# A decoder kernel whose feed-forward is prepared inside the two stages before it: first weights unpacked and turned there, x normalised batch by batch

## The reference, cut to what matters

```python
x = x + L0_attn(layernorm(x), ...)              # 16 heads of 32, one shared K and V
x = x + L0_xattn(layernorm(x), ctx_1024, ...)   # "the mixing"
x = x + L0_ffn(layernorm(x), gate_up_packed, gate_up_scales, down_packed, down_scales)

def L0_xattn(x, ctx, Wq, bq, Wk, bk):
    query = einsum('bnc,dc->bnd', ctx, Wq) + bq
    key = einsum('bnc,dc->bnd', ctx, Wk) + bk
    attention = softmax(einsum('bnd,bmd->bnm', query, key), axis=-1)
    return einsum('bln,bmn->blm', x, attention)

def L0_ffn(x, gate_up_packed, gate_up_scales, down_packed, down_scales):
    # packed: int32 with 8 four-bit floats each; scales: float16 [in/128, out]
    w_gu = dequant_fp4(gate_up_packed, gate_up_scales)     # [2816, 512]
    w_down = dequant_fp4(down_packed, down_scales)         # [512, 1408]
    gate, up = split(x @ w_gu.T, 1408)
    y = (silu(gate) * up) @ w_down.T
    return y / sqrt(mean(y * y, axis=-1) + EPS)
```

## Time and profile before

| what | value |
|---|---|
| median of 3 runs | 2740.32 us (2739.88 to 2743.84) |
| the profiled execution | 2736.73 us, of it span 2735.0 us |
| mean granted clock of TensorE | 0.952 |
| PE, busy in the span | 2459.4 us (90%) |
| DVE | 1747.2 us (64%) |
| ACT | 1212.6 us (44%) |
| POOL | 157.9 us (6%) |

### The profile page before, as it was taken

How to read it: one execution, slowest core, us unless ns; L and a number is a source line. 1 busy time by engine, 2 the same in 40 slices (tenths; PEclk the granted TensorE clock), 3 DMA queues, 4 the chain that set the end, 5 groups by cost and what they waited for, 6 DMA issues and landing times. The chain is left out here.

```text
span 2735.0 us, 39447 instructions
## 1 busy us (share of the span) xinstructions
PE 2459.4 (90%) x11412; PEld 1779.8 (65%) x11412; DVE 1747.2 (64%) x3684; ACT 1212.6 (44%) x2343; POOL 157.9 (6%) x265
## 2 busy tenths in 40 slices
PE   7999977679999769899999599999999999999579
PEld 5554445457777657654446477777777777777457
DVE  6677756668888662266664666676667666666643
ACT  3566654223333332266663344444444444444321
POOL 0000000010000000100003101010100101010100
PEclk9999998879999979989999799999999999999789
DMA  5522100000000023343320100000000000000101
GB/s 164 167 70 69 52 0 0 17 1 1 0 0 0 4 102 114 120 112 92 84 54 0 54 9 19 4 15 4 15 12 8 12 12 15 4 8 0 40 1 62
DMA packets 71459, 103.69 MB, mean 38 GB/s; under 512 B 14447, under 2 KB 27514, under 8 KB 71262
## 3 DMA queue, kind: packets, MB, share of 16 engines
q1 hardware_dynamic: 71390, 102.82, 12.8%
HBM read 72.90 MB, written 29.88 MB: 38 GB/s over the span
## 5 line engine op out<-in xcount | busy, mean ns | idle before, releaser
L2673 DVE SCALAR_TENSOR_TENSOR x_res<-xa_out_bank,xa_den,x_res 128x512 f32 (+1 forms) x256 | 191.5, 748 | 157.2 <-PE xa_out_bank L2313 157.2
L2582 ACT ACTIVATE xa_pT_hi<-xa_t_bank 128x512 fp32r<-128x512 f32 x256 | 149.5, 597 | 124.8 <-PE xa_t_bank L2450 124.8
L2593 ACT ACTIVATE xa_prob<-xa_prob,xa_nmax 128x512 f32<-128x512 f32 x256 | 182.9, 717 | 30.0 <-DVE xa_nmax L2655 30.0
L2313 PE MATMUL xa_out_bank<-xa_o_w,xa_o_hi 128*128 128x512 f32 x512 | 173.1, 419 | 22.5 <-DVE x_res L2673 20.9
L2637 DVE TENSOR_TENSOR xa_pT_lo<-xa_t_bank,xa_pT_hi 128x512 fp32r<-128x512 f32 x256 | 175.7, 687 | 22.7 <-ACT xa_pT_hi L2582 18.6
L2655 DVE CUSTOM_DVE_ANT_0 xa_prob<-xa_s_bank,xa_mask_bias 128x512 f32<-128x512 f32 x256 | 171.1, 687 | 20.1 <-PE xa_s_bank L2313 10.1
L585 DVE TENSOR_REDUCE l1s_mx<-l1s_max_bank 128x1 f32<-128x512 f32 x256 | 156.3, 682 | 13.2 <-PE l1s_max_bank L447 13.2
L1722 DVE SCALAR_TENSOR_TENSOR ffn_yT<-ffn_y,ffn_ysc,ffn_yT 128x512 f32<-128x512 f32 x176 | 129.3, 748 | 48.9 <-PE ffn_y L1494 48.7
L585 DVE TENSOR_REDUCE l0s_mx<-l0s_max_bank 128x1 f32<-128x512 f32 x256 | 156.0, 682 | 2.8 <-PE l0s_max_bank L447 2.7
L2450 PE MATMUL xa_t_bank<-ident,xa_prob 128*128 128x128 f32 x1024 | 149.8, 274 | 0.1
L572 ACT ACTIVATE l1s_pT<-l1s_score_bank 128x512 f32<-128x512 f32 x256 | 140.0, 601 | 16.3 <-PE l1s_score_bank L466 14.8
(11 more groups left out here) (447 smaller groups left out, 5905.9 us busy)
## 6 DMA issues: line engine op xcount, KB each, us to landing
l0s_q<-l_q SPq DMA_DIRECT2D x96, 128.0 KB, 2.4
l1s_q<-l_q SPq DMA_DIRECT2D x96, 128.0 KB, 3.1
l1s_k<-l_k SPq DMA_DIRECT2D x96, 128.0 KB, 3.3
l0s_k<-l_k SPq DMA_DIRECT2D x96, 64.0 KB, 2.4
x_res<-in_x_dram SPq DMA_DIRECT2D x4, 1024.0 KB, 9.8
l_q<-l_q_hi SPq DMA_DIRECT2D x16, 256.0 KB, 2.6
l_q<-l_q_lo SPq DMA_DIRECT2D x16, 256.0 KB, 3.3
l_q<-l1p_hi SPq DMA_DIRECT2D x16, 256.0 KB, 2.1
```

Of the source, the lines that this page charges most:

```text
L2313: last = pe.matmul(bank, w, x, start=(m == 0), stop=(m == len(pairs) - 1))
L2582: act.activation(pT_hi[:, kt % (QT - 1), :], t_bank[kt % 2][:], ACT.Copy).then_inc(pT_hi_done, 1)
L2593: act.activation(prob[:, q, :], prob[:, q, :], ACT.Exp, bias=nmax[:, q:q + 1], scale=-1.0, accum_out=den[:, r, 0, q:q + 1]).then_inc(exp_d ...
L2673: dve.scalar_tensor_tensor(xt, out_bank[:], den[:, r, 2, q:q + 1], xt, ALU.mult, ALU.add)\
```

## The change

It touches everything from the attention's start to the end of the feed-forward's chunk 0, and nothing behind.

- The feed-forward has no preparation stage. Its packed weights are loaded by SP during the attention's projections. Its scales are loaded turned, element by element, by eight DMAs in ACT's own instruction stream, ahead of the first exponential: four of 128x22 and four of 128x11 two-byte values. The 48 small products and the casts are gone.
- Chunk 0 is unpacked by DVE in the attention: four instruction pairs in each of the head pairs 2 to 5 (they cover magnitudes and signs), exponents and scale tables at pair 24, values at 25, signs put in at 29; ACT scales the weights at pairs 26 to 28. For this the last group of six is written out too (`written_out=1`). DVE also takes the statistics of the mixing's first batch at pair 27.
- The ten jobs that turn the mixing's context and weights stand in the free maximum slots of pairs 30 and 31; DVE takes both parts of them (`take_both`).
- The mixing turns chunk 0's weights in its first projections. DVE takes three maxima as soon as the low parts are done, then the first addition, then the fourth maximum, and only then the statistics. Between its low parts it unpacks chunk 1 (batches 0 and 1), takes statistics for the feed-forward (batches 2 and 3) and normalises its first batch (batch 3), which PE turns between the last mixes.
- In the feed-forward, batches 1 to 3 of x are normalised and turned inside chunk 0, each during the batch before. The statistics of the last 8 tiles are taken at the end of chunk 0's batch 0. DVE waits for POOL's zeroing of `ffn_yT` before its first chunk.
- In the projections x is loaded first, the turning of x is dealt out differently (`AFTER`), and the first maxima come earlier.

The diff, cut to its core:

```diff
+        turns = NP // R - self.written_out
         for s in range(R):
             body(s, s)
-        with eng.Fori(1, NP // R) as j:
+        with eng.Fori(1, turns) as j:
             for s in range(R):
                 body(R * j + s, s)
-        for p in range(NP // R * R, NP):
+        for p in range(turns * R, NP):
...
+    def load_scales(self, act, gate_up, down, loaded):
+        for k in range(KC):
+            act.dma_start(self.gu_raw[:, k, :], gate_up[k].rearrange("(f p) -> p f", p=P),
+                          allow_slow_non_contiguous=True).then_inc(loaded, 16)
...
+            act.dma_start(self.dn_raw[:, :, o], down[:, o * P:(o + 1) * P].rearrange("c p -> p c"),
+                          allow_slow_non_contiguous=True).then_inc(loaded, 16)
...
+                pk.load(sp, gate_up_packed, down_packed, pk_loaded)
...
                 att.rows(act, 0, 0)
-                att.scalar(act)
+                take(B - 1, NF - 1)
+                pk.load_scales(act, gate_up_scales, down_scales, pk_scales_loaded)
...
+                def turn_context(n):
+                    if n % 8 >= len(fa_jobs) // 2:
+                        return
+                    if n == 0:
+                        pe.wait_ge(fa_loaded, 48)
+                        pe.wait_ge(att.max_read, 8 * att.NP)
+                    fa_ring.turn(pe, n // 8 * (len(fa_jobs) // 2) + n % 8)
+                att.tensor(pe, turn_context)
...
+                    elif p == last - 8:
+                        dve.wait_ge(pk_mag_in, 1)
+                        pk.exponents(dve).then_inc(pk_mag, 1)
+                        dve.wait_ge(pk_scales_loaded, 16 * 2 * KC)
+                        pk.make_scales(dve, pk_scales_made)
+                    elif p == last - 7:
+                        dve.wait_ge(pk_scales_made, 3)
+                        pk.column_scales(dve, 0).then_inc(pk_csc, 1)
+                        dve.wait_ge(pk_mag, 1)
+                        pk.values(dve).then_inc(pk_f, 1)
+                    elif p == last - 5:
+                        st.fa_norm.stats(dve, 0, batch_tiles(0))
+                    elif p == last - 3:
+                        dve.wait_ge(pk_scaled, 1)
+                        dve.wait_ge(pk_sgn, 1)
+                        pk.put_signs(dve).then_inc(pk_ready, 1)
...
+                        energies(b + 1, 1)
+                        energies(b + 1, 2)
+                    mix(b, 0)
+                    if more:
+                        energies(b + 1, 3)
...
+                def ahead(b, i):
+                    if b == 0:
+                        last = pk.unpack(dve, 1, 0, (i,))
+                        if i == 7:
+                            last.then_inc(mag_in, 1)
+                    elif b == 1:
+                        last = pk.unpack(dve, 1, 1, (i,))
+                        if i == 7:
+                            last.then_inc(sgn_ready, 1)
+                    elif b == 2 and i < QT:
+                        pk.norm.tile_stats(dve, i)
+                    elif b == 2 and i == 7:
+                        pk.norm.combine(dve, 0, batch_tiles(0))
+                    elif b == 3 and i == 1:
+                        dve.wait_ge(mag_in, 1)
+                        pk.exponents(dve).then_inc(mag_ready, 1)
+                    elif b == 3 and i == 3:
+                        pk.column_scales(dve, 1).then_inc(csc_ready, 1)
+                        dve.wait_ge(mag_ready, 1)
+                        pk.values(dve).then_inc(f_ready, 1)
+                    elif b == 3 and i == 5:
+                        pk.norm.scales(dve, 0)
+                        for q in range(QT):
+                            pk.norm.normalise(dve, q)
...
+                            maximum(b + 1, q)
                         add(b, 0)
+                        maximum(b + 1, 3)
+                        norm.stats(dve, b, batch_tiles(b + 1))
...
-                pe.wait_ge(s32_ready, 2)
-                for f in range(2 * NC):
-                    pe.matmul(gu_bank[:, f * KC:(f + 1) * KC], s32[:, f * P:(f + 1) * P], st.ident[0:KC, 0:KC],
-                              start=True, stop=True)
-                for o in range(KC):
-                    last = pe.matmul(dn_bank[:, o * NC:(o + 1) * NC], d32[:, o * P:(o + 1) * P], st.ident[0:NC, 0:NC],
-                                     start=True, stop=True)
-                last.then_inc(s_turned, 1)
...
+                    if isinstance(c, int) and c == 0 and b and n == 0 and m0 == 0:
+                        pe.wait_ge(ring.lo_done, QT * b)
...
+                            elif known and c == 0 and b < B - 1:
+                                pe.wait_ge(norm.xn_ready, QT * b + t + 1)
+                                ring.turn(pe, QT * b + t)
...
+                pe.sem_inc(turned, 3)
...
+                            normalise(1)
+                        elif first and b < B - 1:
+                            if b == 1:
+                                norm.scales(dve, 0)
+                            normalise(b + 1)
...
+                            norm.stats(dve, 0, slice(2 * QT, T))
+                        if b == 0 and more and not first:
...
-                magnitudes(0)
-                exponents(0)
-                values(0)
-                signs(0)
-                put_signs(0)
-                for n in range(2):
-                    take_lo(0, 0, n)
-                magnitudes(1)
-                exponents(1)
-                dve.wait_ge(y_zero, 3)
...
+                norm.scales(dve, None, batch_tiles(1))
+                dve.wait_ge(y_zero, 1)
```

More of the change, by code:

```diff
@@ L575, in step @@
                 self.rows(act, p + 1, (s + 1) % self.R)
+            if beside and isinstance(p, int):
+                beside(p)
         self.rounds(act, step)
@@ L626, in step @@
                 self.split_max(dve, p + 2, s)
+            elif beside:
+                beside(p - self.NP + 2)
             if not self.early(p, 2):
                 self.add_out(dve, p - 2)
+            if ahead and isinstance(p, int):
+                ahead(p)
         self.rounds(dve, step)
@@ L744, in stats, with tile_stats, combine @@
     def stats(self, dve, g, tiles):
+        for t in range(tiles.start, tiles.stop):
+            self.tile_stats(dve, t)
+        self.combine(dve, g, tiles)
+    def tile_stats(self, dve, t):
+        self.last_stats = dve.bn_stats(self.bn[:, t, :], self.st.x[:, t, :])
+    def combine(self, dve, g, tiles):
         self.groups[g] = tiles
         bn, mv = self.bn[:, tiles, :], self.mv[:, :, tiles]
-        for t in range(tiles.start, tiles.stop):
-            last = dve.bn_stats(self.bn[:, t, :], self.st.x[:, t, :])
-        self.link(dve, last)
+        self.link(dve, self.last_stats)
         mean_e, m2_e, mean_o, m2_o = (bn[:, :, k] for k in (1, 2, 4, 5))
@@ L1216, in _ @@
                     if more:
-                        for q in range(1, QT):
-                            energies(b + 1, q)
-                    for t in range(QT):
+                        energies(b + 1, 1)
[3 more added lines that the diff above has]
+                        energies(b + 1, 3)
+                    else:
+                        turn_next(0)
+                        turn_next(1)
+                    mix(b, 1)
+                    if not more:
+                        turn_next(2)
+                        turn_next(3)
+                    for t in range(2, QT):
                         mix(b, t)
-                        if t == 1 and b + 2 < B:
-                            turn_context(b + 2)
             @block.scalar
@@ L1608, in chunk @@
                         take_h(c, b)
[L1609 removed]
+                        if b == 0 and first:
+                            norm.root(act, 0, slice(2 * QT, T))
+                        elif b == 0 and more:
                             scale_weights(c + 1)
@@ L1625, in keep @@
                     square(t, kept[t])
-                act.wait_ge(y_zero, 3)
-                scale_weights(0)
-                for n in range(3):
-                    take_hi(0, 0, n)
-                chunks(act, chunk)
+                chunk(0, 0)
+                with act.Fori(0, (NC - 2) // 2) as j:
+                    chunk(2 * j + 1, 1)
+                    chunk(2 * j + 2, 0)
+                for c in range((NC - 2) // 2 * 2 + 1, NC):
+                    chunk(c, c % 2)
                 for t in range(KEPT, T):
```

513 lines of the change are left out of this document (315 added, 198 removed).

## The result

The changed kernel takes 2706.93 us (median of 4 runs, 2703.71 to 2707.32) against 2740.34 for the kernel before, 33.4 us less. The ratio of the means of the runs is 0.9873, with a 95% interval of 0.9861 to 0.9885. Its profiled execution took 2706.85, with a span of 2705.1 and a mean clock of 0.956. Forecast were 2698.5 and 41.8 us less; the time lies inside both ranges of the prediction.

The account below looks back on a forecast made before the run. TensorE, busy 90% of the span, was taken as the bound. -44.1 - 14.4 + 3 + 1.7 + 12 = -41.8 gave 2694.9 us from 2736.73, 2698.5 as a median; own range 2686 to 2712, stated 2678 to 2724.

Parts of the forecast that it names:

- A: Feed-forward entry: preparation stage gone (66.3 us), chunk 0 takes on 22.2 us of added work and waits; -44.1 us.
- Both stops: TensorE's waits in chunk 0: 5.5 us for POOL's zeroing before batch 1, 6.9 for eight tiles' statistics before batch 2.
- clock term: Chunk 0: products at the lower clock level cost 3.2 us, less 1.3 that the old entry paid; 1.9 us.
- B: Mixing: earlier entry, TensorE's idle gone by new order, last batch gains work; -14.4 us, bounds -20 and -7.
- The forecast's 5.5: Mixing's last batch gains values (1.75), normalising (1.92), four turned tiles (2.1) and statistics; +5.5 us.
- The idle of 5.93 us per batch: Mixing: TensorE's wait until ACT frees the first energy bank was to go, with the maxima ahead of the statistics.
- C: Attention: context turned in pairs 30 and 31; +3 us, bounds 1 and 8.
- D: Attention: DVE's extra work hides in 2.03 us idle per pair, except the statistics at pair 27; +1.7 us.
- E: Attention's start: ACT held by eight scale-load issues before its first exponential; +12 us, bounds +1.4 and +50.
- Both of the forecast's ways: Pricing of the scales' loads: 13.8 us in proportion to SyncE's issue, or 16.6 to 18.7 by packet rate.
- Rival 2: Scales' loads: two-byte values cost 30 to 45 ns per engine, holding ACT about 36 us; 2721 us, chance 0.15.
- F: Projections: x loaded first and turned in another pattern, SP issues two packed loads; 0, between -1 and +1 us.

Follow-up runs that it names:

- e5: Changed kernel, but VectorE waits for GpSimd's zeroing only before its first addition in chunk 0, not before normalising batch 1: 2706.45 us (0.9869).
- e9: Changed kernel with the mixing's order undone whole: statistics before maxima and first addition after them on VectorE, fourth energy before first mix on TensorE: 2720.09 us (0.9924).
- e4: Changed kernel with the next batch's statistics moved back ahead of the three maxima in the mixing's first three batches: 2713.51 us (0.9901).
- e1: Changed kernel without the eight loads of the scales; VectorE sets the raw scales to 1.0 instead: 2686.16 us (0.9807).
- e2: Changed kernel with the eight loads of the scales issued by SyncE instead of ScalarE: 2689.34 us (0.9817).
- e3: Changed kernel, but SyncE starts the loads of context and packed weights only when the scales have landed: 2698.75 us (0.985).
- e8: Changed kernel with scales loaded by SyncE, chunk 0's first three batches written instead of added, and both lumps of statistics spread: 2682.41 us (0.9781).
- e10: Changed kernel with scales loaded by SyncE and chunk 0's first three batches written instead of added, statistics left as they were: 2685.06 us (0.9793).
- e11: e10 with four of chunk 0's eight tiles of statistics taken in the mixing's last batch instead: 2680.14 us (0.9779).
- e7: Changed kernel with statistics cut up: in chunk 0 behind batches 0 and 1, in the attention at pairs 26 and 27: 2710.68 us (0.9892).

## Why the prediction was right, and where it was off

- **A, the preparation: right in sum, with terms that offset each other.** -41.8 by the trace for -44.1. Both stops that it named are there (4.47 and 6.52 us). Its 1.7 for the low parts and the normalising in batch 2 stands against 1.50 and 1.41 us, it had no term for the 1.50 ahead of batch 1 and the 1.46 ahead of batch 3, and it charged more than the turning took: at the full clock a tile's four blocks take TensorE 0.36 us (531.82 to 532.18), by an estimate from that 4.3 us for 12 tiles and not 6.2. No row of before shows the 3.2 and 1.3 us of its clock term. In the changed kernel the granted clock was 0.57 from 520 to 532 us and 0.54 from 545 to 548, and products then followed each other at 0.43 us instead of 0.23, which by an estimate from those steps cost 4 us. That VectorE waits through the zeroing was right in size and wrong in cause: I charged the added wait, and e5 shows that the zeroing itself holds VectorE. The trace of before had it in view, 6.82 us for an unpacking instruction beside the zeroing that else takes 0.27.
- **B, the mixing: right in sum, partly by luck.** -14.1 for -14.4. The entry and the three batches gave 2.6 us more than forecast and the last batch cost 2.8 more (8.3 for 5.5), and the two cancel. The forecast's 5.5 does not follow from the terms that it lists, which come to 5.8 before the statistics, nor its -3.3 from -5.5 and 2.4. The idle of 5.93 us per batch did go, and e9 gives the order's share, 13 to 15.5 us (three batches of about 5), as charged. I put all on VectorE's order; of the 15.5 us that come back in e9 only 3.7 come back in e4, where the statistics alone are moved. The rest came back only with TensorE's order undone too.
- **C and D: right in size.** +2.5 for +3, +1.1 for +1.7; all unpacking is hidden. Which wait makes pairs 30 and 31 longer was not tested.
- **E, the loads of the scales: the step that was mis-sized.** The mechanism stands (e1: 18 to 21 us when they go; e2: 17.6 when another engine issues them). Both of the forecast's ways, 13.8 us of issuing in proportion to SyncE's 1.26 us and 16.6 by 15.7 ns a value, priced the loads with nothing beside them, and for that they were near: e3, where context and packed weights wait, has 14.3 us of issuing, and its first exponential is 9.5 us later than before. The measured issuing is 24.1 us, and the first exponential 19 us later for the forecast's 12. Two small slips change nothing: its lower bound of +1.4 is 1.1 (eight issues at 0.33 less 1.5), and its lowest time of 2678 is 2680. The missing 9.9 us are the context and the packed weights moving at the same time, the first a row that the trace of before had, the second a part of the change. The trace does not agree with the Trainium skill where "DMA: Bandwidth & Descriptors" ("Issuing engines are not separate DMA queues") says that the sequencer's time for starting a transfer is usually small: here it was 24.1 us for 34 KB, until four fifths of the packets had gone.
- **Rival 2 had the wrong mechanism, and 2721 was not met.** It asked for 30 to 45 ns per value for two-byte values as such; in e3 the queue needs 14.7 ns, and the small packets of the earlier trace rows took 15.7. With the other loads beside it the mean over the drain was 24 ns.
- **F is not told from 0.** Without ScalarE's loads the first exponential starts at 96.9, 96.5, 97.1, 95.7 and 95.4 in e1, e2, e8, e10 and e11, instead of 97.41 in the one execution of before: 0.4 to 2.0 us earlier, with a spread of 1.7 between executions whose code is the same up to there but for who issues the loads.

## What to carry to other kernels

A load made of single elements costs its issuer most of the time in which the queue drains it, so its place is an engine that nobody waits for; price it as values per DMA engine by the rate in a row of the trace, and then by what else runs in that stretch. A wait that stands beside another engine's long instruction should be tested by taking the instruction away, not the wait. When work is moved into idle time, two small lumps are better than one only if both gaps have room: four more tiles of statistics fitted the 3.2 us in the mixing's last batch (e11), and behind chunk 0's batch 1 there was no room for them (e7). When a sum comes out right, its terms should still be compared one by one; in the mixing two misses of 2.6 and 2.8 us cancelled.

## What the runs showed of the hardware

- A GpSimd zeroing of 128 x 8192 values (6.9 us) stopped VectorE in the middle of its own short instructions: 5.58 us for a copy that else takes 0.17. A reciprocal (0.18) and a scalar_tensor_tensor (0.16) of four columns, inside the same zeroing, were not held. The Trainium skill ("SBUF — State Buffer", "Terms") says that VectorE and GpSimd share a pair of ports, and that the loser blocks for the whole of the other's instruction; the copy's and the normalising's numbers agree.
- The queue of two-byte values fell from 3993 packets in 4 us to 817 while the other queue moved 1214.
- An engine issuing single-element loads was released with about 3200 of 17024 packets still to come.
- TensorE's granted clock at the attention's start differed between executions with the same code there (1.00 in e2, 0.66 in e10, from 95 to 105 us), and the 2 us were not won back in the attention.
